# Maxima over pairs of PSUM banks in layer 0 of a two-layer cross-attention model, and a re-placed plan

## The chip, the core and the metric

One core of a Trainium2 chip runs the whole model. The metric is the device time of one launch in microseconds. TensorE (PE) multiplies, VectorE (DVE), ScalarE (ACT) and GpSimd (POOL) work on vectors, and SyncE's queue (SP) issues the transfers.

## The reference

`x` is 16 batches of 256 rows of 128; the context is 16 batches of 1601 rows. Two layers run one after the other, each with 16 heads of 8:

```python
x = x + self_attention(x)          # layer 0: causal; layer 1: given mask
x = x + cross_attention(x, ctx)    # 256 queries, 1601 keys; layer 1: given mask
x = x + mixture(x)                 # 8 experts, top 2, 128 -> 512 -> 128
# attention: softmax(q @ k.T / sqrt(8)) @ v, for each head
```

Layer 0 uses layer norms and exact GELU, layer 1 RMS norms, SiLU and one shared expert more.

## The kernel before

**What is computed where.** Every attention needs, for each query and head, the largest score, before the exponential. So the kernel computes the cross scores twice. First come the *maxima*: steps of kind MC, with queries in the 128 partitions. One matmul of 32 contraction rows gives the scores of one head, 128 queries and 512 keys: one full PSUM bank (`chunk_maxima`, L832). VectorE reduces that bank to one number per query (`vector_program`, L1075 in layer 0; in layer 1 a custom operation at L1081 adds the mask as well, followed by a read of its accumulator). The 1601 keys are three chunks of 512 and a tail of 68; a tail step holds both halves of the queries (L1077). A group of four heads has 2 x 3 x 4 = 24 full steps and 4 tails; four groups make a batch. NR (L1085) reduces the chunks to one maximum, NC (L908, L1068) turns it and puts it into a spare row of the query tensor, so that the second computation gives score minus maximum.

Second come the *scores*: a beat of four SC steps (four heads, keys in the partitions, L943, two matmuls each), which ScalarE exponentiates (L1232), and the sums WV (L961), 16 matmuls with the values. A group has 7 such beats, a batch 28.

**Row groups and waves.** The four heads of a group lie at partitions 0, 32, 64 and 96. Matmuls of different heads run side by side in TensorE, so a *wave* of several MC steps takes hardly longer than one. Heads come in the order 2, 3, 0, 1.

**Banks.** Seven PSUM banks, each a tensor of its own, are shared by everything; the eighth holds the sums. A step waits until the last reader of its bank is done (`wait_empty`).

**The plan.** Nothing is dynamic: before the program is emitted, `weave` lays out one order for all engines. A *round* t computes the scores of batch t and, beside them, as side work, the maxima, keys (KC, L990), values (VC, L996), projections (QP, L856) and self-attention (MS, SS) of batch t+1, the loads for t+2, and the experts (EF L1022, ES L1034) of batch t-1. Rounds 0 to 15 are layer 0's, 16 to 31 layer 1's. `WHEN` gives each kind of side work a begin and an end as fractions of `LENGTH`. At each step `weave` tries the head of every list on `Model`, a model of the engines' times, and takes the one with the least planned idle time plus `NEAR` times its place plus `HEAVY` times the backlog.

Maxima are no list of their own. Two places pull them: behind every beat of scores or self-attention, as many steps as the model finds free banks, at most `MOST` = 3, on condition that they are free within `SOON` (such steps are *led* and belong to that beat's wave); and, where `behind` says that the maxima lag the scores, one more beat of up to three after the scores' piece, whether the banks are free or not. `place` gives a step the bank that is free first. Every engine then runs its steps in that order; VectorE's ring of tiles is read in order of issue.

**The queue SP** issues the key moves KD (L1347, 12 transfers a group, 48 a batch), the experts' weights (L1359, two slots), contexts (L1325), masks (L1355), inputs (L1320) and stores (L1364), each after a wait for its buffer.

## Time and profile before

| | us |
|---|---|
| median of 3 runs | 4735.49 |
| lowest and highest | 4720.38, 4739.81 |
| profiled execution, span from first to last instruction | 4733.2 |
| TensorE, VectorE, ScalarE, GpSimd busy | 4551.8, 3608.6, 2701.6, 698.8 |
| mean granted clock of TensorE | 0.980 |

The time of the profiled execution as a launch is not given apart from its span, so what lies around the span is not known. In a group row, "busy" is the time in which at least one instruction of the group ran, "mean ns" the mean duration of one (overlapping ones count in full), and the last part tells how long the engine idled just before them and what ended it. In a timeline row, neighbouring instructions of one line are merged.

### The profile page before, as it was taken

The page shows a single profiled execution, that of the slowest core. Times are in us where ns is not written, and L with a number is a line of the kernel's source. Part 1 is how long each engine was busy: PE and PEld are TensorE (multiplying, and loading weights), DVE is VectorE, ACT ScalarE, POOL GpSimd, SP SyncE. Part 2 cuts the span into 40 slices and gives each one's busy share as a digit, 9 for nine tenths or more (in the row PEclk, how much of TensorE's full clock was granted, in tenths as well). Part 3 has the DMA queues.
Part 4 walks back from the last instruction along what each step waited for, and adds up shares of the span by engine and source line. Part 5 has one row for each costly group of instructions (what it writes and reads, how often), then busy time and mean ns, then how long its engine had stood idle before and what let it go on. Part 6 is the DMA issues. An engine that isn't in the chain of part 4 may idle for free.

```text
span 4733.2 us, 104936 instructions
## 1 busy us (share of the span) xinstructions
PE 4551.8 (96%) x40946; PEld 2800.6 (59%) x41312; DVE 3608.6 (76%) x9823; ACT 2701.6 (57%) x5505; POOL 698.8 (15%) x853
## 2 busy tenths in 40 slices
PE   6999999999999999999999999999999999999999
PEld 3566555666655566665565556655566555655566
DVE  6867777777777777777768887788877888788875
ACT  1666666667666666665565555555555555555554
POOL 2111211211121121111110111011110111101100
PEclk8999999999999999998999999999999999999999
DMA  2222222222222222223233323332233323333222
GB/s 68 39 60 57 44 55 56 63 67 56 60 46 53 55 65 67 53 58 80 55 97 81 83 61 87 96 86 68 66 99 82 86 61 83 103 81 80 62 70 74
DMA packets 168008, 327.22 MB, mean 69 GB/s; under 512 B 25656, under 2 KB 76624, under 8 KB 167520
## 3 DMA queue, kind: packets, MB, share of 16 engines
q1 hardware_dynamic: 167184, 320.48, 27.6%
q8 instruction: 333, 5.46, 0.5%
q14 instruction: 155, 1.27, 0.1%
q10 hardware_dynamic: 336, 0.01, 0.0%
HBM read 237.40 MB, written 4.19 MB: 51 GB/s over the span
## 4 chain that ended last, share of the span: by engine, by line
PE 79%; DVE 14%; ACT 3%; issue 2%; SPq 1%; DMA 0%; POOL 0%; DVEq 0%
PE sums L961 16%; PE b L1022 10%; PE b L1034 10%; PE b L832 9%; PE b L943 7%; PE b L933 7%; DVE chunk_max L1075 5%; PE b L856 4%; PE b L917 3%; DVE nm_s L1064 3%; DVE b L1081 3%; PE b L884 2%; PE b L996 2%; PE b L908 2%; ACT probs_c L1232 1%
## 5 line engine op out<-in xcount | busy, mean ns | idle before, releaser
L1232 ACT ACTIVATE probs_c<-b 128x512 f32<-128x512 f32 (+1 forms) x3584 | 1738.8, 571 | 1069.0 <-PE b L943 1061.2
L1081 DVE CUSTOM_DVE_ANT_0 b<-b,mcross_q 128x512 f32<-128x512 f32 (+1 forms) x2048 | 1121.8, 605 | 211.2 <-PE b L832 208.9
L1075 DVE TENSOR_REDUCE chunk_max<-b 128x1 f32<-128x512 f32 x1536 | 973.6, 683 | 144.3 <-PE b L832 139.3
L961 PE MATMUL sums<-probs_c,vc 128*32 128x256 f32 x13312 | 932.4, 395 | 0.6 <-ACT o_c L1236 0.3
L832 PE MATMUL b<-kc,qc 32*128 32x512 f32 (+1 forms) x4096 | 820.5, 412 | 18.2 <-DVE chunk_max L1075 7.1
L1034 PE MATMUL b<-w_back,hidden 128*128 128x128 f32 x4352 | 562.3, 280 | 14.7 <-DVE vc L1138 9.2
L832 PEld LDWEIGHTS b<-kc,qc 32*128 32x128 f32 x4096 | 425.3, 187 | 250.9 <-ACT probs_c L1232 94.4
L1034 PEld LDWEIGHTS b<-w_back,hidden 128*128 128x128 f32 x4352 | 526.4, 192 | 73.3 <-ACT probs_c L1232 24.4
L961 PEld LDWEIGHTS sums<-probs_c,vc 128*32 128x32 f32 x13312 | 348.0, 111 | 341.1 <-issue 168.0
L943 PE MATMUL b<-qc,kc 32*128 32x256 f32 (+1 forms) x6656 | 514.4, 336 | 16.7 <-DVE chunk_max L1077 2.2
L1022 PE MATMUL b<-xT_e,w_in 128*128 128x256 f32 x2176 | 527.9, 387 | 0.8 <-DVE chunk_max L1081 0.7
L1214 DVE SCALAR_TENSOR_TENSOR xe<-b,comb,xe 128x128 f32<-128x128 f32 x544 | 188.0, 349 | 405.3 <-PE b L1034 404.3
L943 PEld LDWEIGHTS b<-qc,kc 32*128 32x128 f32 (+1 forms) x6656 | 302.4, 182 | 300.2 <-issue 185.0
L1227 ACT ACTIVATE probs_s<-b 128x512 f32<-128x512 f32 x512 | 277.8, 594 | 308.1 <-PE b L895 305.7
L1022 PEld LDWEIGHTS b<-xT_e,w_in 128*128 128x128 f32 x2176 | 396.7, 191 | 88.1 <-ACT probs_c L1232 25.4
L933 PE MATMUL b<-mcross_k,ident_b 128*128 128x512 bf16 (+1 forms) x1569 | 403.1, 363 | 32.8 <-ACT probs_s L1227 11.1
L1064 DVE TENSOR_REDUCE nm_s<-b 128x2 f32<-128x512 f32 x512 | 328.5, 684 | 31.2 <-PE b L889 31.1
L1081 DVE DVE_READ_ACCUMULATOR2_ANT chunk_max<- 128x1 f32 x2048 | 290.7, 142 | 0.0
L933 PEld LDWEIGHTS b<-mcross_k,ident_b 128*128 128x128 bf16 (+1 forms) x1792 | 169.1, 99 | 201.5 <-DVE chunk_max L1081 37.9
L1207 DVE SCALAR_TENSOR_TENSOR hidden<-hidden,b 128x512 f32<-128x512 f32 x288 | 193.6, 686 | 101.4 <-ACT hidden L1255 101.4
L1307 POOL TENSOR_TENSOR rstd_s<-mean_var_s,halves 128x2 f32<-128x2 f32 x32 | 23.2, 724 | 1607.6 <-DVE mean_var_s L1122 1607.6
L1251 ACT ACTIVATE hidden<-b,b_hid 128x256 f32<-128x256 f32 x512 | 207.1, 474 | 88.5 <-PE b L1022 86.3
(159 smaller groups left out, 4498.6 us busy)
## 6 DMA issues: line engine op xcount, KB each, us to landing
w_in<-in_experts SPq DMA_DIRECT2D x272, 256.0 KB, 3.2
w_back<-in_experts SPq DMA_DIRECT2D x272, 256.0 KB, 3.3
kc<-k_hi SPq DMA_DIRECT2D x1024, 50.0 KB
ctxT<-in_ctxT SPq DMA_DIRECT2D x32, 800.5 KB, 6.2
kc<-k_lo SPq DMA_DIRECT2D x512, 50.0 KB
mask_words<-in_mcross SPq DMA_DIRECT2D x32, 800.5 KB
mask_words<-in_mcrossT SPq DMA_DIRECT2D x32, 768.0 KB
out_x<-xe SPq DMA_DIRECT2D x32, 128.0 KB, 1.9
```

Source lines behind the costliest of these rows:

```text
L832: last = pe.matmul(tile[:, n * y.kn:(n + 1) * y.kn], T["qc"][y.p][rows, y.g, qt * P:(qt + 1) * P], T["kc"][rows, y.g, y.k0:y.k0 + y.kn], s ...
L933: pe.matmul(tile_of(T, y)[0:y.kn, 0:n * S], T["ident_b"][0:y.kn, 0:y.kn], mask, start=True, stop=False)
L943: last = pe.matmul(tile_of(T, y)[0:y.kn, half * S:(half + 1) * S], T["kc"][rows, y.g, kt * P:kt * P + y.kn], T["qc"][y.p][rows, y.g, :], s ...
L961: last = pe.matmul(acc[HP * j:HP * j + HP, :], T["vc"][x.p][0:x.kn, v0:v0 + HP], probs_of(T, x)[0:x.kn, j, half:half + S], start=x.j == 0, ...
L1022: last = pe.matmul(tile[:, half * S:(half + 1) * S], T["w_in"][load.slot][:, f * P:(f + 1) * P], T["xT_e"][:], start=True, stop=True)
L1034: last = pe.matmul(tile[:, 0:D], hid[:, f, x.c * P:(x.c + 1) * P], T["w_back"][load.slot][:, f * D:(f + 1) * D], start=f == 0, stop=f == N ...
L1064: dve.tensor_reduce(maxima[:, x.j, :, MROW], tile.rearrange("p (q k) -> p q k", q=QT), AX, ALU.max, negate=True).then_inc(M["d_read"], 1)
L1075: done = dve.tensor_reduce(best[:, x.i:x.i + 1], tile, AX, ALU.max)
L1081: done = dve.tensor_tensor_reduce(part, part, mask, 1.0, -3e38, ALU.add, ALU.max, best[:, qt:qt + 1])
L1227: act.activation(T["probs_s"][:, x.j, :], tile, ACT.Exp, scale=SCALE).then_inc(M["a_read"], 1)
L1232: act.activation(probs_of(T, x)[0:x.kn, x.j, 0:n], tile[0:x.kn, 0:n], ACT.Exp, scale=SCALE).then_inc(M["a_read"], 1)
L1251: done = act.activation(T["hidden"][x.i % 2][:, f, :], tile[:, half * S:(half + 1) * S], ACT.Gelu, bias=T["b_hid"][:, x.i, f:f + 1])
```

## The change

In layer 0 an MC step covers two heads, 2 and 3 or 0 and 1, in two neighbouring banks: two matmuls of different row groups, and one reduction over both banks that writes two maxima; a tail step makes four matmuls and, still, two reductions. A group has 12 full steps and 2 tail steps for 24 and 4. All seven banks become one PSUM tensor, so that an instruction can address two of them. The planner counts tiles rather than steps: `MOST` becomes 4 tiles, for both layers; a led pair needs two free neighbours (`pairs_in`); `place` looks for two neighbouring banks; a pull made because nothing else can go on takes at most two tiles. Within a wave the matmuls go round by heads. Layer 1 keeps one bank a step (`TWO_BANKS` is false for it, and what is written for `WIDE` isn't reached). `LENGTH` of layer 1 goes from 145.8 to 130.4, `HEAVY` from 0.091 to 0.096, and the fractions of `WHEN` change in both layers; `SLACK` is 2 steps of 28 as before, now as a share.

```diff
+TWO_BANKS = (True, False)
...
-LENGTH = (140.4, 145.8)
+LENGTH = (140.4, 130.4)
...
     def place(self, x):
 
         taken = {n for y in x.beat[:x.beat.index(x)] for n in y.banks} if x.led else ()
-        return [min((n for n in range(BANKS) if n not in taken), key=lambda n: max(self.pe, self.banks[n]))]
+        width = tiles_of(x)
+        runs = [range(n, n + width) for n in range(BANKS - width + 1)]
+        return list(min((some for some in runs if not any(n in taken for n in some)),
+                        key=lambda some: max(self.pe, *(self.banks[n] for n in some))))
...
-NEAR, AHEAD, SOON, MOST, SLACK = 0.0436, 167.5, 0.32, 3, 2
-HEAVY, DRY = 0.091, 0
+NEAR, AHEAD, SOON, MOST, SLACK = 0.0436, 167.5, 0.32, 4, 0.07
+HEAVY, DRY = 0.096, 0.0000
...
-                more = plan.pull(model, pending, min(MOST, len(free)))
+                more = plan.pull(model, pending, min(MOST, len(free)), room=free)
...
+def maximum_us(x):
...
+    if TWO_BANKS[x.l]:
+        return 1.07 if x.c < CHUNKS else 0.45
+    return (0.6, 0.65)[x.l] if x.c < CHUNKS else 0.3
...
+def parts_of(x):
...
+    tails = x.c == CHUNKS
+    return [(x.j + n, qt, n * BANK + tails * qt * x.kn, x.k0, x.kn) for qt in (range(QT) if tails else [x.i])
+            for n in range(tiles_of(x))]
...
+                heads = (2, 0) if TWO_BANKS[l] else (2, 3, 0, 1)
...
-    def pull(self, model, pending, most, late=False):
-
-        out = []
-        while len(out) < most and self.groups:
+    def pull(self, model, pending, most, late=False, room=None):
+
+        out, taken = [], 0
+        while self.groups:
             x = self.groups[0][0]
+            taken += tiles_of(x)
+            if taken > most or taken > 2 and late:
+                break
             needs = [y for name, y in x.of.items() if name != "mask"]
+            if tiles_of(x) > 1 and room is not None and pairs_in(room) < len(out) + 1:
+                break
...
-WHEN = [{"experts": (0.207, 1.0), "keys": (0.177, 0.426), "values": (0.198, 0.975), "self": (0.08, 0.58), "load": (0.358, 1.0), "context": (0.95, 1.0)},
-        {"experts": (0.079, 1.0), "keys": (0.293, 0.368), "values": (0.119, 0.401), "self": (0.029, 0.629), "load": (0.5, 0.656), "context": (0.49, 0.668), "cross masks": (0.393, 0.779), "self masks": (0.786, 0.796)}]
+WHEN = [{"experts": (0.207, 1), "keys": (0.157, 0.426), "values": (0.313, 0.975), "self": (0.077, 0.577),
+         "load": (0.368, 0.988), "context": (0.929, 0.939)},
+        {"experts": (0.079, 1), "keys": (0.282, 0.368), "values": (0.119, 0.37), "self": (0.029, 0.584),
+         "load": (0.378, 0.623), "context": (0.469, 0.661), "cross masks": (0.333, 0.692),
+         "self masks": (0.772, 0.786)}]
...
+    turns = [(y, n) for n in range(len(parts_of(maxima[0]))) for y in maxima] if even else [
+        (y, n) for y in maxima for n in range(len(parts_of(y)))]
...
+            last = pe.matmul(T["psum"][:, first:first + kn], T["qc"][y.p][head_rows(j, HP), y.g, qt * P:(qt + 1) * P],
+                             T["kc"][head_rows(j, HP), y.g, k0:k0 + kn], start=True, stop=True)
...
+                heads = tiles_of(x)
+                two = T["psum"][:, first:first + heads * BANK].rearrange("p (j n) -> p j n", j=heads)
+                best = T["chunk_max"][:, x.g % 2, :, x.j:x.j + heads, x.c].rearrange("p q j -> p j q")
+                if tails:
+                    for j in range(heads):
+                        done = dve.tensor_reduce(best[:, j, :], two[:, j, 0:QT * TAIL].rearrange("p (q k) -> p q k", q=QT),
+                                                 AX, ALU.max)
+                else:
+                    done = dve.tensor_reduce(best[:, :, x.i], two, AX, ALU.max)
...
-        "banks": [psum(f"b{n}", [P, BANK]) for n in range(BANKS)],
+        "psum": psum("pool_of_banks", [P, BANKS * BANK]),
```

## Rows read from the trace of the kernel before

**Rows 1.** The page's head and its first part: busy time, share, instructions.

```profile
span 4733.2 us, 104936 instructions
...
PE 4551.8 (96%) x40946; PEld 2800.6 (59%) x41312; DVE 3608.6 (76%) x9823; ACT 2701.6 (57%) x5505; POOL 698.8 (15%) x853
```

**Rows 2.** Windows of 13 rounds of each layer: busy (count), PEclk, DMA share, GB/s.

```profile
349.00:2154.30 1805.30, 1744.35 (x15882) 1088.77 (x15947) 1325.74 (x2918) 1180.68 (x2394) 318.53 (x378) 0.97 0.25 57
2461.00:4426.90 1965.90, 1922.91 (x17404) 1170.82 (x17639) 1598.83 (x5048) 1013.22 (x2082) 245.27 (x313) 1.00 0.32 81
```

**Rows 3.** Windows of single rounds, two of layer 0 and the last.

```profile
630.20:766.80 136.60, 132.32 (x1225) 82.99 (x1230) 101.82 (x225) 90.78 (x185) 24.49 (x29) 0.99 0.26 58
905.00:1044.90 139.90, 135.49 (x1225) 84.11 (x1230) 102.11 (x225) 90.83 (x186) 24.48 (x29) 0.96 0.25 57
2154.30:2309.30 155.00, 147.58 (x1239) 91.73 (x1244) 109.63 (x276) 91.22 (x186) 26.18 (x34) 0.89 0.31 79
```

**Rows 4.** Windows around one dip of the clock.

```profile
919.00:922.40 3.40, 2.94 (x17) 1.64 (x13) 3.30 (x9) 0.13 (x1) 0.00 (x0) 1.00 0.00 0
...
925.90:929.20 3.30, 3.30 (x30) 2.36 (x32) 2.29 (x8) 1.41 (x3) 0.00 (x0) 0.51 0.00 0
```

**Rows 5.** The chain, 349 to 2154.3, by line.

```profile
by line: PE sums L961 17.1%; PE b L832 11.8%; PE b L1034 10.8%; PE b L1022 10.4%; DVE chunk_max L1075 9.6%; PE b L943 8.1%; PE b L856 4.3%; PE b L917 3.2%; DVE nm_s L1064 2.8%; PE b L884 2.0%; PE b L908 2.0%; PE b L996 1.9%; ACT probs_s L12
```

**Rows 6.** Groups by line and form, 349 to 2154.3: busy us, mean ns, idle before.

```profile
L1075 DVE TENSOR_REDUCE chunk_max<-b 128x1 f32<-128x512 f32 x1248 | 791.4, 683 | 110.1 <-PE b L832 105.5
...
L832 PE MATMUL b<-kc,qc 32*128 32x512 f32 x1249 | 323.2, 466 | 5.4 <-DVE chunk_max L1075 3.5
...
L1077 DVE TENSOR_REDUCE chunk_max<-b 128x2 f32<-128x136 f32 x208 | 52.9, 294 | 21.4 <-PE b L832 21.3
```

**Rows 7.** Waits of TensorE's loads, 349 to 2154.3: total us, times, longest.

```profile
PEld b L832 <- DVE chunk_max L1075: 47.5, 130, 0.5
...
PEld b L943 <- DVE chunk_max L1075: 16.3, 47, 0.4
PEld b L996 <- DVE chunk_max L1075: 14.8, 39, 0.4
```

**Rows 8.** VectorE's timeline from 1037 us: start, us, count.

```profile
1041.55 2.48 DVE L1075 TENSOR_REDUCE chunk_max<-b 128x1 f32<-128x512 f32 x4 [0.30 <-PE b L832]
...
1045.47 1.29 DVE L1075 TENSOR_REDUCE chunk_max<-b 128x1 f32<-128x512 f32 x2
```

**Rows 9.** TensorE's timeline in layer 1.

```profile
2900.29 0.39 PE L832 MATMUL b<-kc,qc 32*128 32x512 f32 x1
2900.61 1.07 PE L961 MATMUL sums<-probs_c,vc 128*32 128x256 f32 x16
2901.61 0.50 PE L832 MATMUL b<-kc,qc 32*128 32x512 f32 x4
2902.04 2.94 PE L1034 MATMUL b<-w_back,hidden 128*128 128x128 f32 x24
```

**Rows 10.** TensorE's timeline in layer 0.

```profile
968.12 0.72 PE L832 MATMUL b<-kc,qc 32*128 32x512 f32 x3
968.77 1.07 PE L961 MATMUL sums<-probs_c,vc 128*32 128x256 f32 x16
...
971.75 0.49 PE L832 MATMUL b<-kc,qc 32*128 32x512 f32 x1 [0.27 <-DVE chunk_max L1075]
```

**Rows 11.** The first and the last wave of those counted (690 with them).

```profile
349.45 0.63 PE L832 MATMUL b<-kc,qc 32*128 32x512 f32 x3
...
2152.45 0.50 PE L832 MATMUL b<-kc,qc 32*128 32x512 f32 x1
```

**Rows 12.** Waits of SP's queue, whole execution.

```profile
SPq L1359 <- PE b L1034: 491.5, 113, 10.5
...
SPq L1347 <- DVE chunk_max L1075: 341.7, 17, 25.4
```

**Rows 13.** DMA issues: size, median us to landing.

```profile
ctxT<-in_ctxT SPq DMA_DIRECT2D x32, 800.5 KB, 6.2
```

More of the change, by code:

```diff
@@ L59 @@
 TAIL = 68
+TWO_BANKS = (True, False)
+WIDE = 802
 CHUNKS = SK // BANK
@@ L210, in read @@
             idle = max(0, second - max(self.dve, made))
-            self.dve = max(self.dve, made, second) + (0.3 if kind == "MC" and x.c == CHUNKS else self.cost(DVE_US, x))
+            self.dve = max(self.dve, made, second) + (maximum_us(x) if kind == "MC" else self.cost(DVE_US, x))
             done = self.dve + PASS
@@ L253, in add @@
                 n = [y for y in x.beat if y.kind == "MC"].index(x)
-                self.pe = self.run(begin, WAVE if n % HG else 0.22 + (0.1 if first_wave else 0), 0.053)
+                wave = 0.34 if tiles_of(x) > 1 and x.l else 0.22
+                whole = HG // 2 if tiles_of(x) > 1 else HG
+                self.pe = self.run(begin, WAVE if n % whole else wave + (0.1 if first_wave else 0), 0.21 / whole)
             elif x.kind in ("SC", "MS", "SS"):
@@ L380, in __init__ @@
         self.at = {}
-        self.waiting, self.groups, self.follow, self.pulled = [], [], [], 0
+        self.waiting, self.groups, self.follow, self.pulled, self.share = [], [], [], 0, {}
         self.model = Model()
@@ L531, in pull @@
             out.append(self.groups[0].pop(0))
-            self.pulled += 1
+            self.pulled += self.share[id(out[-1])]
             if self.groups[0][0].kind == "NR":
@@ L537, in behind @@
     def behind(self, x):
-        steps = QT * HG * CHUNKS + HG
-        return self.pulled < steps * (self.batch * NG + x.g + 1 + (x.i + 1) / (KP - 1.5)) - SLACK
+        return self.pulled < self.batch * NG + x.g + 1 + (x.i + 1) / (KP - 1.5) - SLACK
     def scores(self, l, p, g, kp):
@@ L815, in tile_of @@
 def tile_of(T, x):
-    return T["banks"][x.banks[0]][:]
+    return T["banks"][x.banks[0]]
 def chunk_maxima(pe, T, M, x):
-    for y in x.beat:
-        if y.kind != "MC":
-            continue
-        if y is not x:
-            wait_empty(pe, M, y)
-        if "q" in y.of:
-            pe.wait_ge(M["q_made"], nth(y.of["q"]))
-            pe.wait_ge(M["kc_moved", y.g], 16 * MOVES * y.of["moved"].c)
-        tile, rows = tile_of(T, y), head_rows(y.j, HP)
-        for n, qt in enumerate([y.i] if y.c < CHUNKS else range(QT)):
-            last = pe.matmul(tile[:, n * y.kn:(n + 1) * y.kn], T["qc"][y.p][rows, y.g, qt * P:(qt + 1) * P],
-                             T["kc"][rows, y.g, y.k0:y.k0 + y.kn], start=True, stop=True)
-        last.then_inc(M["d_made"], 1)
+    maxima = [y for y in x.beat if y.kind == "MC"]
+    even = len({len(parts_of(y)) for y in maxima}) == 1
+    turns = [(y, n) for n in range(len(parts_of(maxima[0]))) for y in maxima] if even else [
+        (y, n) for y in maxima for n in range(len(parts_of(y)))]
+    if maxima:
+        for y, n in turns:
+            parts = parts_of(y)
+            if n == 0:
+                if y is not x:
+                    wait_empty(pe, M, y)
+                if "q" in y.of:
+                    pe.wait_ge(M["q_made"], nth(y.of["q"]))
+                    pe.wait_ge(M["kc_moved", y.g], 16 * MOVES * y.of["moved"].c)
+            j, qt, begin, k0, kn = parts[n]
+            first = y.banks[0] * BANK + begin
+            last = pe.matmul(T["psum"][:, first:first + kn], T["qc"][y.p][head_rows(j, HP), y.g, qt * P:(qt + 1) * P],
+                             T["kc"][head_rows(j, HP), y.g, k0:k0 + kn], start=True, stop=True)
+            if n == len(parts) - 1:
+                last.then_inc(M["d_made"], 1)
 def tensor_program(pe, T, M, order):
@@ L1071, in vector_program @@
                 dve.wait_ge(M["masks_made"], nth(x.of["mask"]))
-            some = [(x.i, tile)] if x.c < CHUNKS else [(qt, tile[:, qt * TAIL:(qt + 1) * TAIL]) for qt in range(QT)]
+            tails = x.c == CHUNKS and x.kn == TAIL
             best = T["chunk_max"][:, x.g % 2, :, x.j, x.c]
-            if x.l == 0 and x.c < CHUNKS:
-                done = dve.tensor_reduce(best[:, x.i:x.i + 1], tile, AX, ALU.max)
-            elif x.l == 0:
-                done = dve.tensor_reduce(best, tile[:, 0:QT * TAIL].rearrange("p (q k) -> p q k", q=QT), AX, ALU.max)
-            else:
-                for qt, part in some:
+            first = x.banks[0] * BANK
+            if x.l == 0:
+                heads = tiles_of(x)
[5 more added lines that the diff above has]
+                                                 AX, ALU.max)
+                else:
+                    done = dve.tensor_reduce(best[:, :, x.i], two, AX, ALU.max)
+            else:
+                for n, qt in enumerate(range(QT) if tails else [x.i]):
+                    part = T["psum"][:, first + n * x.kn:first + (n + 1) * x.kn]
                     mask = T["mcross_q"][x.p][:, qt, x.k0:x.k0 + x.kn]
@@ L1441, in program @@
         "pick": sb("pick", [P, QT, E0]), "comb": sb("comb", [P, QT, E0 + 1]), "combT": sb("combT", [E0, S]),
-        "banks": [psum(f"b{n}", [P, BANK]) for n in range(BANKS)],
+        "psum": psum("pool_of_banks", [P, BANKS * BANK]),
         "sums": psum("sums", [P, BANK]),
     }
+    T["banks"] = [T["psum"][:, n * BANK:(n + 1) * BANK] for n in range(BANKS)]
     for role in "se":
```

25 lines of the change are left out of this document (21 added, 4 removed).

## The prediction

> **What bounds the kernel now.** I read the page first, for the load of the engines: TensorE is busy 96% of 4733.2 us, VectorE 76% [rows 1]. A busy share doesn't say what TensorE's time consists of, so next I cut the execution into rounds (one batch's pass through one layer), using the fourth `o_c` copy of each batch as the mark. Thirteen steady rounds of layer 0 take 1805.3 us, 138.9 each, at a granted clock of 0.97; thirteen of layer 1 take 1965.9, 151.2 each, at 1.00 [rows 2]. So layer 0, where the new operation goes, is about 16 x 139 = 2222 us of the whole. Single rounds of layer 0 come in kinds: 136.6 us at clock 0.99, 139.9 at 0.96, and the round that prepares layer 1 takes 155.0 at 0.89 [rows 3]. Work and order are nearly the same in them, so some 3 us of a round hang on the clock. It falls in short stretches from 2.4 to 1.2 GHz: from 925.9 to 929.2 it is 0.51 of full speed, some us after a stretch in which TensorE had gaps (busy 2.94 of 3.40 us) [rows 4].
>
> Then I read who ends TensorE's time. In layer 0's chain the maxima's reduction L1075 holds 9.6%: 173 us of 13 rounds, 13.3 a round [rows 5]. It is busy 791.4 us there, 60.9 a round [rows 6], so about 22% of it lies on the path. TensorE's loads wait for it at many lines: 47.5 us in 130 waits before L832, 16.3 before the scores L943, 14.8 before L996 [rows 7]. Summed over those three, 6 us a round. TensorE is the bound, and it is held up by banks that VectorE hasn't freed; most of the rest is its own work.
>
> **The change, part by part.** A round of layer 0 has 96 full tiles (16 batches: 1536 reductions in all) and 16 tails.
>
> (a) *The reduction.* 96 reductions of 512 become 48 of 2 x 512; the 16 tail reductions stay (two operations a step). The trace has no read over two banks. In a run, single reductions follow each other every 0.60 us: four end in 2.48, two in 1.29 [rows 8]. The slope is (683 - 294) ns over (512 - 136) elements [rows 6], 1.035 ns each, so 512 more cost 530 ns: a pair costs 1.13 us in a run where two singles cost 1.20. VectorE gains 0.07 x 48 = 3.4 us a round. Bounds: crossing banks costs as much as starting anew or more (2 x 683 ns = 1.37 us, a loss of 8 us a round), or the whole fixed part of an instruction vanishes (294 - 136 x 1.035 = 153 ns, a gain of 7.3). I take 0.07, since the slope comes from the same operation on the same memory. With 22% on the path: **-0.75 us a round**.
>
> The rows show a fixed part for each instruction. The Trainium skill (Advanced Engine Details and Errata, TRN2 Errata) speaks of a bubble between instructions and says that one instruction may read several PSUM banks; VectorE: DVE Perf Modes, in its section on the errata, gives 120 cycles and one per element at 0.96 GHz for a read of PSUM, by which the pair saves 125 ns, 6.0 us a round for 3.4; on the path that would be another 9 us over 16 rounds. The trace's 683 ns stands beside that page's 658.
>
> (b) *Fewer waves.* Tiles of different row groups run side by side: a wave of four lasts 0.50 us and the next work begins 0.43 after its start, and the shortest step, with a wave of one, is 0.32 (2900.29 to 2900.61) [rows 9]; I take 0.33 for a wave. In the 13 rounds I counted 570 waves of full tiles (156 of one, 153 of two, 236 of three, 25 of four or five) and 120 of tails, the first at 349.45 and the last at 2152.45 [rows 11]; 324 follow scores, 129 follow self-attention's beats, 104 follow the sums L961. That is 44 + 9 = 53 waves a round. After the change a round has 56 steps of two tiles. Behind the 28 beats of scores, which hold four of seven banks, at most one pair fits, and only if two neighbours are free; before, 93 of those 324 waves found only one tile, so I give a pair to 60%: 17. Of the 10 self-attention beats I give 5 one. The other 34 steps go where the plan is behind, two pairs at a time: 17 waves. So 39 waves for 53: 14 x 0.33 = **-4.6 us a round**.
>
> (c) *Waits for banks.* Those two-pair waves need four of seven banks, each pair as neighbours, and they stand in TensorE's fixed order: behind one that waits are the next sums or experts, and behind those ScalarE's and VectorE's next tiles. There are 9 more such waves than the 8 now after L961. The nearest row is the wait of L832's load for a reduction, 47.5/130 = 0.37 us [rows 7]: **+3.3 us a round**. Bounds: 0, when the banks happen to be free, and a whole pair's 1.13 on each of the 17. Against that, the third tile of a wave often came late (968.12, a wave of three lasts 0.72 us against 0.50 for a wave of four [rows 9, 10]); such delay averages 0.20 us in the 129 three-tile waves behind scores, 2.0 us a round. A pair waits too, for its later bank, so I take half: **-1.0**.
>
> (d) *Layer 1* keeps its custom operation on one bank; only the limit of three tiles becomes four where the plan is behind. It has 143 waves behind L961 in 13 rounds, 11 a round; one more tile in each takes about 4 waves of three away: -1.3 us. The fourth bank must be waited for at one or two of the eleven (0.37 each): **-0.8 us a round**, with bounds -1.3 (no wait) and +2.8 (a wait at each, 4.1, less 1.3).
>
> (e) *Side work at other places.* Instruction counts stay: 4 key steps, 5 value steps, and masks and loads as before. The key move's 48 DMA issues a batch and the loads share SP's queue. SP waits long there already (L1347 for the maxima: 341.7 us in 17 waits; L1359 for the experts' matmuls: 491.5 in 113) [rows 12], and a DMA releases TensorE in none of the costly waits (the three of [rows 7] are VectorE's), so moved loads cost nothing while they stay a few us ahead. What queues behind a waiting load on SP is the next expert's weights, which have two slots. The context load of layer 0 moves to 0.929 but stays behind the last value step; it lands in 6.2 us [rows 13], and the next keys start at 0.157 of a round, 22 us later. Should that cover go, the price is up to those 6.2 us a round, behind KC and everything on TensorE. Layer 1's length 130.4 for 145.8 mainly scales all its places, and weighs planned idle time more against them. What these moves do to the waits and to the clock I can't read from rows: 0, with bounds from the two kinds of rounds: all at 136.7 us is -2.2 a round, all at 139.9 +1.0 [rows 3]; for layer 1 +-1.5 (1%, an estimate from the spread of layer-0 rounds, since its own are even).
>
> The sum: layer 0 -0.75 - 4.6 + 3.3 - 1.0 = -3.05 a round, x 16 = -49 us; layer 1 -0.8 x 16 = -13 us. The profiled execution has 4733.2 us of span, and what lies around it isn't shown; the median of the runs is 2.3 above it. 4733 - 62 + 2 = **4673 us**, 1.3% faster.
>
> **Rivals.** *Slower: the pairs starve the banks.* From seven single banks VectorE's work becomes three pairs and a leftover, and a pair comes free only when both halves are read. Scores take four singles, often one of each pair, and so leave no neighbours. For it: TensorE already waits 0.37 us a time for these readers, and the window at 971.75 shows a single tile after an idle 0.27 for L1075 [rows 10]. Against it: a pair in a run is freed no later than the second single was. It decides from a mean wait of w with 17w = 3.0 (the 8 waits now) + 4.6 + 1.0 + 0.75, w = 0.55 us. At 0.8 us layer 0 is +4.3 a round, +68 us; with layer 1 unhelped or delayed by up to 1.5 a round: 4800 to 4825. On top come clock losses: at 0.96 all over, +16. The skill's Perfetto Trace Analysis, Matmuls, asks that independent groups rotate through different banks so that evacuation overlaps; holding two at once goes against that; no row here shows a pair held, so it isn't decided.
>
> *No change:* pairs are pulled one at a time, so 53 waves stay about 50; (b) and (c) shrink to nothing, and what is left is 0.75 x 16 = 12 us and some of layer 1: 4715 to 4735. For it: TensorE is 96% busy and most of the waves cost it only a third of a us.
>
> *The change doesn't do what it says:* the read over two banks costs two reads, 1.20 to 1.37 us. Then VectorE works up to 8 us a round more, at 22% +1.8, and layer 0 gains about 1: 4715.
>
> *Better than forecast:* new places also remove the stretch after the router (from 968.77 to 971.75 TensorE has one set of sums and then waits for L1075 [rows 10]) and keep the clock up: another 2.2 x 16 = 35 us, and some of the 155.0 us round: 4620 to 4640.
>
> **How the numbers follow.** Forecast 0.46, better 0.10, no change 0.16, two reads 0.06, starved banks 0.22. About 0.5% (24 us) is what a measurement of this kernel can tell from no change. Most of the forecast and all of the better case lie beyond it: faster 0.55; the no-change and two-read cases and the rim of the forecast's: same 0.22; starved banks and a rest of unlucky places: slower 0.23. The range goes from the better case to the lower part of the starved one: 4615 to 4800. The likeliest case alone spans 4635 to 4710.
>
> **What would show it.** A pair near 1.2 us alone and 1.13 in a run; 768 of them; the share of L1075's successor in layer 0's chain below 9.6%; about 40 waves a round, many of four tiles; L832's busy time in 13 layer-0 rounds well below 323 us for full tiles; rounds near 136 us in layer 0 and 150 in layer 1. Wrong would be: waits before L832's successor above 0.55 us a time, more than 50 waves, rounds above 139, or a layer 1 that moves more than layer 0.

## The result and the profile after

The changed kernel takes 4958.27 us (median of 4; 4936.48 to 4988.18) against 4734.83: **slower by 4.8%**, ratio 1.0479, 95% interval 1.0433 to 1.0524. The profiled execution took 4988.18 us, its span is 4986.6. The page's head and busy row:

```profile
span 4986.6 us, 104446 instructions
...
PE 4665.8 (94%) x40938; PEld 2808.5 (56%) x41312; DVE 3562.2 (71%) x9055; ACT 2701.8 (54%) x5505; POOL 687.3 (14%) x853
```

VectorE works 46 us less than before, as meant; TensorE's share falls from 96% to 94%. Cut into the same rounds as [rows 2], with the fourth `o_c` copy as the mark:

```profile
378.00:2377.40 1999.40, 1850.64 (x15870) 1111.67 (x15939) 1288.61 (x2293) 1181.38 (x2393) 316.00 (x378) 0.91 0.23 52
2695.30:4677.80 1982.50, 1917.76 (x17404) 1159.38 (x17638) 1596.01 (x5046) 1011.54 (x2081) 236.19 (x314) 1.00 0.31 81
```

A layer-0 round takes 1999.4/13 = 153.8 us for 138.9, at a granted clock of 0.91 for 0.97; a layer-1 round 152.5 for 151.2. Of the 253 us between the two spans, the first 378 us (349 before) hold 29, these 13 rounds of layer 0 hold 194 and the 13 of layer 1 hold 17; the rest lies between and behind the windows. The chain of layer 0, against [rows 5]:

```profile
by line: PE sums L1023 14.4%; DVE chunk_max L1146 13.7%; PE pool_of_banks L893 9.6%; PE pool_of_banks L1084 9.3%; PE pool_of_banks L1096 9.3%; PE pool_of_banks L1005 8.3%; ACT probs_c L1303 4.9%; PE pool_of_banks L918 4.4%; DVE nm_s L1126 2
```

The reduction has grown from 9.6% of 1805 to 13.7% of 1999, from 13 to 21 us a round, though it is busy less. The groups, against [rows 6]:

```profile
L1146 DVE TENSOR_REDUCE chunk_max<-pool_of_banks 128x2 f32<-128x1024 f32 x623 | 742.8, 1222 | 255.5 <-PE pool_of_banks L893 254.2
...
L893 PE MATMUL pool_of_banks<-kc,qc 32*128 32x512 f32 x1246 | 263.0, 530 | 41.6 <-DVE chunk_max L1146 24.1 <-DVE k_lo L1203 5.7 <-ACT probs_c L1303 3.4
...
L1143 DVE TENSOR_REDUCE chunk_max<-pool_of_banks 128x2 f32<-128x136 f32 x208 | 51.3, 294 | 63.2 <-PE pool_of_banks L893 63.2
```

A pair takes 1222 ns, and TensorE's time in full maxima tiles fell from 323.2 to 263.0 us. I counted the waves as before: 488 for 690 in 13 rounds, 37.5 a round for 53, of which 195 have two tiles and 195 have four. The maxima got cheaper on TensorE, then, and the loss is where something else waits. The waits of layer 0 name it, against [rows 7]:

```profile
PEld pool_of_banks L1005 <- DVE chunk_max L1146: 72.5, 103, 1.6
...
PEld pool_of_banks L893 <- DVE chunk_max L1146: 63.1, 115, 1.0
...
PE pool_of_banks L1005 <- DVE chunk_max L1146: 42.1, 79, 1.2
```

Before, the loads of the scores (L943, now L1005) waited 16.3 us in 47 times for a reduction; now 72.5 in 103, and their matmuls 42.1 more. One such place, in TensorE's timeline and then in VectorE's:

```profile
1206.37 1.13 PE L893 MATMUL pool_of_banks<-kc,qc 32*128 32x512 f32 x4
1207.66 0.38 PE L946 MATMUL pool_of_banks<-causal_k,ident_b 128*128 128x512 bf16 x1 [0.16 <-ACT probs_c L1303]
...
1208.91 0.49 PE L893 MATMUL pool_of_banks<-kc,qc 32*128 32x512 f32 x2 [0.44 <-DVE chunk_max L1146]
...
1209.95 0.50 PE L893 MATMUL pool_of_banks<-kc,qc 32*128 32x512 f32 x2
...
1210.29 0.27 PE L1005 MATMUL pool_of_banks<-qc,kc 32*128 32x256 f32 x1
1211.08 0.50 PE L1005 MATMUL pool_of_banks<-qc,kc 32*128 32x256 f32 x7 [0.52 <-DVE chunk_max L1146]
```

```profile
1207.54 4.62 DVE L1146 TENSOR_REDUCE chunk_max<-pool_of_banks 128x2 f32<-128x1024 f32 x4 [1.74 <-PE pool_of_banks L893]
```

A wave of two pairs is done by 1207.5, and two more pairs follow at 1208.91 and 1209.95. VectorE reads the four pairs in 4.62 us, that is (4.62 - 1.22)/3 = 1.13 from start to start. The beat of scores issues its first matmul at 1210.29 and its second only at 1211.08, just after the third of these reads ends (1207.54 + 1.22 + 2 x 1.13 = 1211.02).

To compare kernels I use one sum, the *scores' time*: from each start of a scores matmul to TensorE's next start, per layer-0 round of the profiled execution. It is 15.6 us before and 25.0 after, +9.4, the largest single term of the 14.9 lost, but not the whole account. The maxima's time, the same sum for their matmuls, fell by 4.8 (25.6 to 20.8), so the rest of TensorE's work makes up the other 10.3. Of that, 3.6 are the sums, 27.9 to 31.5, which hardly ever wait and took longer, at the lower clock. Their rows, before and after:

```profile
L961 PE MATMUL sums<-probs_c,vc 128*32 128x256 f32 x4992 | 351.5, 401 | 0.0
```

```profile
L1023 PE MATMUL sums<-probs_c,vc 128*32 128x256 f32 x4992 | 378.7, 426 | 0.5
```

The windows tell it from the other side. TensorE idles (1805.3 - 1744.35)/13 = 4.7 us a round before and (1999.4 - 1850.64)/13 = 11.4 after. So 6.7 of the 14.9 us are idle time, of which 4.3 stand just before matmuls of the scores (0.7 to 5.0) and 2.7 just before those of the maxima (0.6 to 3.3); the other 8.2 are busy time that has become longer.

### The profile page after: what moved, and what is told of

It reads as the page before. It is cut to its first block, busy times and chain, and to the rows that moved or that the text cites. A ratio compares the mean times of both kernels' runs of the same rounds, so it can differ in the third digit from the quotient of the medians.

```text
span 4986.6 us, 104446 instructions
## 1 busy us (share of the span) xinstructions
PE 4665.8 (94%) x40938; PEld 2808.5 (56%) x41312; DVE 3562.2 (71%) x9055; ACT 2701.8 (54%) x5505; POOL 687.3 (14%) x853
## 3 DMA queue, kind: packets, MB, share of 16 engines
q14 instruction: 149, 1.22, 0.1%
## 4 chain that ended last, share of the span: by engine, by line
PE 68%; DVE 21%; ACT 4%; SPq 3%; issue 2%; DMA 2%; POOL 0%; DVEq 0%
PE sums L1023 14%; PE pool_of_banks L1084 9%; PE pool_of_banks L1096 9%; PE pool_of_banks L893 8%; DVE chunk_max L1146 7%; PE pool_of_banks L1005 7%; PE pool_of_banks L995 6%; DVE pool_of_banks L1151 5%; PE pool_of_banks L918 4%; DVE nm_s L1126 3%; ACT probs_c L1303 3%; SPq L1418 2%; PE pool_of_banks L979 2%; DMA mask_words<-in_mcrossT 2%; PE pool_of_banks L946 1%
## 5 line engine op out<-in xcount | busy, mean ns | idle before, releaser
L1303 ACT ACTIVATE probs_c<-pool_of_banks 128x512 f32<-128x512 f32 (+1 forms) x3584 | 1739.6, 572 | 1352.5 <-PE pool_of_banks L1005 1346.6
L1151 DVE CUSTOM_DVE_ANT_0 pool_of_banks<-pool_of_banks,mcross_q 128x512 f32<-128x512 f32 (+1 forms) x2048 | 1121.8, 605 | 265.0 <-PE pool_of_banks L893 262.8
L1146 DVE TENSOR_REDUCE chunk_max<-pool_of_banks 128x2 f32<-128x1024 f32 x768 | 914.5, 1221 | 327.6 <-PE pool_of_banks L893 325.9
L893 PE MATMUL pool_of_banks<-kc,qc 32*128 32x512 f32 (+1 forms) x4096 | 697.6, 435 | 57.8 <-DVE chunk_max L1146 32.8
L1005 PE MATMUL pool_of_banks<-qc,kc 32*128 32x256 f32 (+1 forms) x6656 | 576.4, 348 | 83.9 <-DVE chunk_max L1146 55.4
L1005 PEld LDWEIGHTS pool_of_banks<-qc,kc 32*128 32x128 f32 (+1 forms) x6656 | 335.2, 188 | 411.7 <-issue 196.9
L1096 PE MATMUL pool_of_banks<-w_back,hidden 128*128 128x128 f32 x4352 | 561.7, 280 | 3.4 <-DVE chunk_max L1151 1.8
L1096 PEld LDWEIGHTS pool_of_banks<-w_back,hidden 128*128 128x128 f32 x4352 | 530.7, 193 | 54.2 <-issue 21.4
L1084 PE MATMUL pool_of_banks<-xT_e,w_in 128*128 128x256 f32 x2176 | 539.1, 393 | 3.3 <-DMA w_in<-in_experts 2.6
L893 PEld LDWEIGHTS pool_of_banks<-kc,qc 32*128 32x128 f32 x4096 | 340.4, 194 | 311.1 <-ACT probs_c L1303 108.3
L1084 PEld LDWEIGHTS pool_of_banks<-xT_e,w_in 128*128 128x128 f32 x2176 | 401.4, 194 | 102.3 <-ACT probs_c L1303 34.1
L995 PE MATMUL pool_of_banks<-mcross_k,ident_b 128*128 128x512 bf16 (+1 forms) x1568 | 409.1, 364 | 47.9 <-DVE chunk_max L1151 17.5
L1378 POOL TENSOR_TENSOR rstd_s<-mean_var_s,halves 128x2 f32<-128x2 f32 x32 | 23.1, 722 | 1685.8 <-DVE mean_var_s L1193 1685.8
```

What stands on the lines that cost most here:

```text
L893: last = pe.matmul(T["psum"][:, first:first + kn], T["qc"][y.p][head_rows(j, HP), y.g, qt * P:(qt + 1) * P], T["kc"][head_rows(j, HP), y.g ...
L995: pe.matmul(tile_of(T, y)[0:y.kn, 0:n * S], T["ident_b"][0:y.kn, 0:y.kn], mask, start=True, stop=False)
L1005: last = pe.matmul(tile_of(T, y)[0:y.kn, half * S:(half + 1) * S], T["kc"][rows, y.g, kt * P:kt * P + y.kn], T["qc"][y.p][rows, y.g, :], s ...
L1084: last = pe.matmul(tile[:, half * S:(half + 1) * S], T["w_in"][load.slot][:, f * P:(f + 1) * P], T["xT_e"][:], start=True, stop=True)
L1096: last = pe.matmul(tile[:, 0:D], hid[:, f, x.c * P:(x.c + 1) * P], T["w_back"][load.slot][:, f * D:(f + 1) * D], start=f == 0, stop=f == N ...
L1146: done = dve.tensor_reduce(best[:, :, x.i], two, AX, ALU.max)
```

## The experiments

| run | ratio to before (95%) | layer 0: us a round, clock | scores' time | layer 1: us a round |
|---|---|---|---|---|
| before | 1 | 138.9, 0.97 | 15.6 | 151.2 |
| changed | 1.048 (1.043-1.052) | 153.8, 0.91 | 25.0 | 152.5 |
| e1 singles | 1.032 (1.029-1.036) | 147.2, 0.94 | 19.2 | 152.9 |
| e2 old places | 1.058 (1.056-1.061) | 154.1, 0.92 | 25.5 | 154.1 |
| e3 new places | 1.021 (1.019-1.024) | 142.1, 0.96 | 16.7 | 154.6 |
| e4 two reads | 1.056 (1.053-1.058) | 154.4, 0.92 | 25.7 | 152.9 |
| e5 four | 1.027 (1.025-1.030) | 142.9, 0.96 | 17.5 | 154.1 |
| e6b one pair behind | 1.151 (1.148-1.153) | 180.0, 0.84 | 25.8 | 156.5 |
| e7 half release | 1.043 (1.041-1.045) | 149.0, 0.95 | 24.1 | 152.5 |
| e8 price | 1.064 (1.061-1.066) | 153.6, 0.92 | 24.9 | 153.2 |
| e9 pairs where they fit | 1.003 (1.001-1.004) | 139.0, 0.98 | 15.9 | 151.3 |
| e10 filler | 1.053 (1.051-1.056) | 153.3, 0.93 | 27.1 | 152.5 |
| e11 two | 1.059 (1.057-1.061) | 151.0, 0.94 | 20.6 | 157.3 |
| e12 spread | 1.027 (1.025-1.029) | 146.2, 0.95 | 22.4 | 152.9 |
| e13 spread, half release | 1.031 (1.028-1.034) | 145.5, 0.96 | 22.1 | 152.5 |
| e14 four, led | 1.017 (1.014-1.020) | 143.7, 0.96 | 17.5 | 151.4 |
| e15 four, behind | 1.020 (1.017-1.024) | 142.9, 0.96 | 18.8 | 153.7 |
| e16 spread, old places | 1.053 (1.050-1.056) | 152.6, 0.89 | 23.1 | 154.5 |
| e17 masks late | 1.084 (1.082-1.087) | 151.6, 0.93 | 24.9 | 164.5 |
| e18 masks early | 1.002 (1.001-1.003) | 138.9, 0.97 | 15.6 | 152.1 |

The ratios come from all runs of a version, against the kernel before in the same session. The us a round, the clock and the scores' time come from one profiled execution each. That of the changed kernel was the longest of its four (span 4986.6, their mean 4958.7), so differences of one or two us a round between rows may be those of single executions.

### Taking the change apart: e1, e2, e3, e5

```diff
e1, in the changed kernel:
-TWO_BANKS = (True, False)
+TWO_BANKS = (False, False)
e2, in the changed kernel:
-LENGTH = (140.4, 130.4)
+LENGTH = (140.4, 145.8)
... and HEAVY and WHEN of before
e3, in the kernel before:
-LENGTH = (140.4, 145.8)
+LENGTH = (140.4, 130.4)
... and HEAVY and WHEN of the change
e5, in the kernel before:
-NEAR, AHEAD, SOON, MOST, SLACK = 0.0436, 167.5, 0.32, 3, 2
+NEAR, AHEAD, SOON, MOST, SLACK = 0.0436, 167.5, 0.32, 4, 2
```

> The changed kernel with one tile a step in layer 0 again (one reduction a bank); the new places, the limit of four tiles and the one PSUM tensor stay. Theory A (pairs starve the banks of the scores): layer-0 rounds fall from 153.8 back to 138 to 142 us, the clock there to 0.96 or more, total 4740 to 4800. Theory B (the new places do the harm): layer-0 rounds stay above 148 us, total above 4880.

> The changed kernel with the places, the layer length and the backlog weight of before; pairs and the limit of four stay. Theory A: layer-0 rounds stay at 150 us or more, total 4920 to 5000, layer 1 near 151 to 152 a round. Theory B: layer-0 rounds fall to 142 or less, total below 4820.

> The kernel before with nothing but the new places, length of layer 1 and backlog weight. Theory A: within 1% of before, 4700 to 4780. Theory B: most of the loss is here already, above 4860.

> The kernel before with a limit of four tiles for three, nothing else. Theory D (it is the number of banks that one wave takes from the scores, not the pair as such): layer-0 rounds 141 to 146 us, the scores' time a round above the 15.6 of before, layer 1 152.5 to 154.5, total 4810 to 4890. Rival (four tiles are harmless one bank at a time): 4710 to 4760.

Measured: e1 4889.67, e2 5011.55, e3 4832.21, e5 4854.28 us. Neither theory stands alone: each of e1, e2 and e3 misses part or all of both theories' ranges, while e5 lies within theory D's in every point. Along one path a layer-0 round goes 138.9, with new places 142.1 (e3), with the limit of four 147.2 (e1), with pairs 153.8 (changed). Along the other, with the limit of four 142.9 (e5), with pairs 154.1 (e2). So pairs cost 6.6 to 11.2 us a round, the limit of four 4.0 to 5.1, the places 3.2 with single tiles. What a part costs depends on the others: with pairs and the limit of four, layer 0 takes the same with the new places as with the old (153.8 and 154.1). The new places suit the pairs' plan: the total with pairs is 53 us better with them than without. e1's load waits for a reduction before the scores lie between both kernels:

```profile
PEld pool_of_banks L1005 <- DVE chunk_max L1146: 45.8, 101, 0.8
```

e3 in the two windows of 13 rounds shows how much a mere re-placing costs in both layers:

```profile
347.20:2193.90 1846.70, 1775.16 (x15939) 1089.72 (x15939) 1323.69 (x2918) 1181.17 (x2393) 318.29 (x378) 0.96 0.24 56
2502.90:4512.60 2009.70, 1950.58 (x17638) 1160.80 (x17642) 1600.68 (x5047) 1012.63 (x2081) 236.82 (x314) 0.99 0.30 80
```

### What a pair does: e4, e7, e9

```diff
e4, in the changed kernel:
-                    done = dve.tensor_reduce(best[:, :, x.i], two, AX, ALU.max)
+                    for j in range(heads):
+                        done = dve.tensor_reduce(best[:, j:j + 1, x.i], two[:, j, :], AX, ALU.max)
e7, on top of e4 (for tails too); wait_empty waits for the count of the bank's own read:
+                        if j:
+                            done.then_inc(M["d_read"], 1)
e9, in the kernel before; banks are one tensor:
+            if x.joined:
+                continue
+            if x.mate:
+                two = T["psum"][:, first:first + 2 * BANK].rearrange("p (j n) -> p j n", j=2)
+                done = dve.tensor_reduce(T["chunk_max"][:, x.g % 2, x.i, x.mate.j:x.j + 1, x.c], two, AX, ALU.max)
```

> The changed kernel, the same order and the same pairs, but each pair read by two reductions of one bank each, the count of reads raised by the second alone. If the read over two banks is slow in itself (theory C): faster than the changed kernel by over 0.5%. Theory A: VectorE pays 0.06 us more a pair, 48 pairs a round, and so up to 1 us a round: total 0 to 20 us above the changed kernel's 4958.

> As the run with two reads for a pair (5000.6 us), the same order, but each of the two reads frees its bank at once. Theory E (a pair's first bank is held for the second's read, and that is what TensorE waits for): 40 us or more off 5000.6, to 4960 or less. Rival (TensorE waits for the last tile of a wave anyway): 4985 to 5010.

> The kernel before with its order of instructions on TensorE unchanged; the seven banks are one PSUM tensor, and where two heads' tiles of one wave can lie in neighbouring banks (177 times) one reduction reads both and frees both. The read itself is then priced without a new plan: VectorE gains 177 x 0.06 = 11 us, of which a fifth may show. All theories that blame the plan or the number of banks: 4715 to 4745, no change. If one tensor or the read over two banks were harmful in itself: above 4755.

Measured: e4 5000.58 us, e7 4934.31, e9 4750.93. The one read beats two by 42 us, twice the expected bound, so theory C falls. (In the table the two differ by only 0.6 us a layer-0 round, since the changed kernel's profiled execution is its longest.) With TensorE's order unchanged, freeing each bank at its own read takes 66 us off e4, 5.4 a layer-0 round, as theory E says. The scores' waits for reductions, e4 first, then e7:

```profile
PEld pool_of_banks L1005 <- DVE chunk_max L1147: 88.8, 124, 1.7
...
PE pool_of_banks L1005 <- DVE chunk_max L1147: 49.1, 82, 1.3
```

```profile
PEld pool_of_banks L1013 <- DVE chunk_max L1159: 56.4, 132, 1.0
...
PE pool_of_banks L1013 <- DVE chunk_max L1159: 19.0, 62, 0.7
```

88.8 + 49.1 becomes 56.4 + 19.0 (the rows of loads and matmuls overlap, so it is their fall that counts). This is the joint release, shown against two reads. The 5.4 us are not all in the scores' time, which fell by 1.6 (25.7 to 24.1); the sums fell by 1.8, and the windows, e4 first, give 12.3 and 9.4 us a round of idle TensorE at clocks of 0.92 and 0.95:

```profile
385.80:2393.50 2007.70, 1847.74 (x15938) 1106.69 (x15937) 1326.27 (x2917) 1183.31 (x2393) 317.40 (x378) 0.92 0.23 52
```

```profile
386.20:2323.20 1937.00, 1814.39 (x15940) 1101.10 (x15939) 1325.81 (x2916) 1182.97 (x2393) 316.76 (x378) 0.95 0.24 53
```

Against the changed kernel, with its one read, e7 gains 24 us, with intervals that overlap. e9 has TensorE's order of before, with the banks of the maxima chosen anew, and 177 pairs in all:

```profile
L1112 DVE TENSOR_REDUCE chunk_max<-pool_of_banks 128x1 f32<-128x512 f32 x984 | 632.8, 683 | 90.0 <-PE pool_of_banks L863 85.1
...
L1110 DVE TENSOR_REDUCE chunk_max<-pool_of_banks 128x2 f32<-128x1024 f32 x132 | 160.8, 1218 | 26.0 <-PE pool_of_banks L863 24.6 <-PE pool_of_banks L939 1.4
```

1218 ns a pair, VectorE busy a little less, and no gain: 15 us slower, 0.13 to 0.43%, just above the range expected. The read is not the harm (e4 says the same for the changed kernel's order), but neither is its saving worth anything here; what costs the 15 us, the read or the other choice of banks, isn't known.

### Smaller waves, and pairs at other places: e6b, e8, e11, e12, e13, e16

```diff
e6b, in the changed kernel, where the plan is behind:
-            steps = plan.pull(model, pending, MOST)
+            steps = plan.pull(model, pending, 3)
e8, in the changed kernel, the planner's price:
-        return 1.07 if x.c < CHUNKS else 0.45
+        return 1.15 if x.c < CHUNKS else 0.52
e11, in the kernel before:
-NEAR, AHEAD, SOON, MOST, SLACK = 0.0436, 167.5, 0.32, 3, 2
+NEAR, AHEAD, SOON, MOST, SLACK = 0.0436, 167.5, 0.32, 2, 2
e12, in the changed kernel:
-        if scores and plan.behind(scores[-1]):
+        plan.latest = scores[-1] if scores else plan.latest
+        pairs = plan.groups and tiles_of(plan.groups[0][0]) > 1
+        if (scores or pairs and plan.latest) and plan.behind(plan.latest):
             follow()
-            steps = plan.pull(model, pending, MOST)
+            steps = plan.pull(model, pending, 3 if pairs else MOST)
e13: e12 on top of e7. e16: e12 with the places, length and HEAVY of before.
```

> The changed kernel, but where the plan is behind it pulls at most three tiles, so one pair in layer 0 instead of two. Theory D: the scores wait less (25.0 us a round falls below 20), layer-0 rounds at most 148, total below 4890. Rival (any pair starves the banks, by its two neighbours): layer-0 rounds stay above 151, total 4930 or more.

> The changed kernel with the planner's price of a pair raised from 1.07 to 1.15 us and of a tail pair from 0.45 to 0.52, near what the trace shows (1.14 from start to start, 0.51). Theory F (the plan is bad because it takes a pair for cheaper than it is): 50 us or more below 4958. Theory D: the price hardly matters, 4920 to 4990.

> The kernel before with a limit of two tiles for three. If only the banks taken from the scores count (theory D alone), layer 0 gets faster: below 138.9 us a round. If there is an optimum, because smaller waves are more waves and the maxima fall behind, rounds go to 141 us or more and the total above 4790. I expect the second.

> The changed kernel, but where layer 0's maxima are behind the plan pulls one pair after every piece of work, scores or not, instead of two pairs after the scores alone. So no wave that isn't led takes four banks, and the slots suffice. Theory D: the scores' time falls from 25.0 to below 20 us a round, layer-0 rounds to 148 or less, total below 4900. Rival (a pair anywhere delays what comes next): total 4930 or more.

> The spread pairs of the run before (4868 us, 146.2 us a layer-0 round), and each pair read by two reductions that free their banks one by one. In the changed kernel's order that was worth 5.4 us a round against two reads with a joint release. Theory E: it is worth 2 to 5 here too, total 4800 to 4845. Rival (with no wave of four tiles, nobody waits for a pair's first half): 4860 to 4890.

> The run with spread pairs (4868 us) with the places, length and weight of before. With two-pair waves the old places cost 53 us against the new, nearly all in layer 1; one tile at a time they save 97. If the new places suit pairs: 4900 to 4950. If they only suit waves of four: below 4850.

Measured: e6b 5435.98 us, e8 5024.71, e11 5018.92, e12 4868.07, e13 4875.43, e16 4982.99. e6b missed on both theories. With one pair behind each beat there are too few places for 56 steps: 26 waves of its 13 rounds hold 8 or 10 full tiles, where the steps left over come one after another, and the maxima themselves become the wait:

```profile
PEld pool_of_banks L893 <- DVE chunk_max L1146: 214.9, 333, 2.1
...
PE pool_of_banks L893 <- DVE chunk_max L1146: 94.9, 143, 2.0
```

310 us in 13 rounds for L893 (loads and matmuls, partly the same time); in the changed kernel the loads waited 63.1. It tells nothing of starved scores, only that pairs need slots. e12 gives the slots with few waves of four: among waves of full tiles alone 51 in 13 rounds for 195, and 8 larger ones. It gets 90 us back, 7.6 a round. The total is as theory D says; the scores' time, 22.4, fell less than the 20 it asked for, as waits moved to the maxima:

```profile
PEld pool_of_banks L895 <- DVE chunk_max L1148: 94.5, 173, 1.5
...
PEld pool_of_banks L1007 <- DVE chunk_max L1148: 41.0, 60, 1.7
...
PE pool_of_banks L895 <- DVE chunk_max L1148: 27.0, 57, 1.3
...
PE pool_of_banks L1007 <- DVE chunk_max L1148: 24.2, 40, 1.4
```

e13 differs from e12 by the half release and by two reads for one, so it stands against e12 as e7 stands against the changed kernel: e7 is 24 us faster, e13 7 us slower (by the ratios 0.5% and 0.3%, both at the rim of the noise). That speaks for a joint release that hurts where four banks are queued for VectorE at once and not among single pairs. It isn't shown: the saving of the one read, 42 us among waves of two pairs, is in both comparisons, and single pairs with two reads and a joint release were not run. e11 shows the other side of the optimum, as expected: with two tiles 65 waves a round and 151.0 us. e8 (a true price made the plan worse by 66 us) rejects theory F, but lies above theory D's 4990 as well: the price mattered, and why isn't known. e16 says that the new places suit pairs, one or two at a time: without them 115 us more, above both ranges.

### Where the fourth tile does its harm: e14, e15

```diff
e14, in the kernel before:
-                more = plan.pull(model, pending, min(MOST, len(free)))
+                more = plan.pull(model, pending, min(4, len(free)))
e15, in the kernel before:
-            steps = plan.pull(model, pending, MOST)
+            steps = plan.pull(model, pending, 4)
```

> The kernel before, with four tiles allowed in the waves that ride on a beat of scores or self-attention, three elsewhere. Three banks at most are free behind a beat of four, so the limit of four rarely bites: 4725 to 4770.

> The kernel before, with four tiles allowed only in the waves of their own that are pulled when the maxima are behind. Theory D puts the 126 us of the limit of four here: 4810 to 4880. Rival (the loss is that of any other order, wherever the fourth tile goes): this and its sister lose about alike.

Measured: 4807.86 and 4826.19 us. I expected next to nothing of e14, and it lost 81 us with waves of almost the same sizes as before:

```profile
356.10:2224.50 1868.40, 1765.95 (x15871) 1089.10 (x15934) 1327.57 (x2919) 1179.70 (x2393) 317.63 (x378) 0.96 0.24 56
```

143.7 us a round in layer 0, layer 1 unhurt. e15 lost 100 us, within both theories' ranges, and 81 + 100 is more than the 126 of e5, so the two places don't add up. Theory D explains at most part of the limit's cost; a slightly other order of layer 0 costs 3 to 5 us a round by itself (e3, e5, e14, e15), at a clock of 0.96 for 0.97. What in those orders does it I haven't found.

### The clock: e10

```diff
in the changed kernel, scores of layer 0:
+                        if not x.last and y in scores[2:]:
+                            pe.matmul(tile_of(T, x)[0:x.kn, 0:S], T["kc"][head_rows(x.j, HP), x.g, kt * P:kt * P + x.kn],
+                                      T["qc"][x.p][head_rows(x.j, HP), x.g, :], start=True, stop=True)
                         wait_empty(pe, M, y)
```

> The changed kernel; in layer 0 TensorE repeats the first matmul of a beat of scores before it waits for the third and the fourth bank (54 repeats of 0.11 us a round, 6 us where nothing hides them). Theory G (TensorE's gaps bring the clock down, and the clock brings 0.6 us per us lost): the clock in layer 0 rises from 0.91 to 0.93 or more, and the total is at most 4975. Rival (the clock doesn't follow such gaps): clock within 0.01 of 0.91, total 4990 to 5050.

Measured: 4989.12 us.

```profile
386.60:2379.20 1992.60, 1857.54 (x16575) 1145.09 (x16574) 1287.12 (x2294) 1181.71 (x2392) 315.16 (x376) 0.93 0.23 52
```

The profiled clock in layer 0 is 0.93, as theory G says, but the total isn't, and it lies 1 us below the rival's range. Over all runs the granted clock of the whole kernel is 0.958 against 0.956, and the time is 31 us longer. So filling these waits in this way doesn't bring the clock back; the rise in layer 0 compares two single executions, of which the changed kernel's has the lowest clock of four. What the clock costs can be read without it, from executions of one kernel that differ in nothing else. The changed kernel's four spans are 4986.6, 4951.0, 4962.3 and 4934.9 us at clocks of 0.947, 0.957, 0.957 and 0.963. Call (1 - clock) x span the lost clock time: a fit within each kernel and session, over all kernels' executions up to e16 (114), gives 0.63 us of span per us lost. The changed kernel loses 218 us on average, the one before 94: 124 x 0.63 = 78 of the 223 us go with the clock, and some 145 would be there at an equal clock. This is an estimate. It carries what goes together within one kernel over to the difference between two, and takes the clock for the cause. In the profiled execution, at 0.947, the same rule gives 107 of its 253 us. What lowers the clock isn't shown by a run of its own; in the table it is mostly lower where rounds are longer.

### Layer 1: e17, e18

The chain of one layer-1 round of the changed kernel passes through the queue SP and a transfer:

```profile
3088.46 1.16 SPq L1418
3089.61 0.04 issue
3089.66 5.14 DMA mask_words<-in_mcrossT
3094.82 0.32 DVE mcross_k L1219
```

In this round the mask's load is issued only once the key moves (L1418) ahead of it in the queue are out. VectorE, which takes its work in order, waits for it, and TensorE's scores behind VectorE:

```profile
3094.82 0.96 DVE L1219 TENSOR_SCALAR mcross_k<-mask_words 128x1536 bf16<-128x1536 int32 x1 [1.22 <-DMA mask_words<-in_mcrossT]
...
3097.34 0.81 PE L995 MATMUL pool_of_banks<-mcross_k,ident_b 128*128 128x512 bf16 x3 [1.12 <-DVE xe L1285]
```

```profile
DVE mcross_k L1219 <- DMA mask_words<-in_mcrossT: 11.3, 13, 2.1
```

```diff
e17, in the changed kernel:            e18, in the kernel before:
-"cross masks": (0.333, 0.692)          -"cross masks": (0.393, 0.779)
+"cross masks": (0.439, 0.871)          +"cross masks": (0.298, 0.619)
```

> The changed kernel with layer 1's cross masks put back to the time of before (0.439 to 0.871 of 130.4 is 0.393 to 0.779 of 145.8). In the changed kernel VectorE waits 0.87 us a layer-1 round for a mask's load, and TensorE's scores wait behind it (9.8 us in 12 of 13 rounds). Theory M (the moved masks make layer 1's 1.3 us): no wait for that load, layer-1 rounds 151.2 to 151.9 instead of 152.5, total 10 to 25 us lower. Rival (the order as a whole): layer-1 rounds 152.3 or more.

> The kernel before with only the cross masks moved ahead to the time of the changed kernel. Theory M: the wait for the mask's load appears, 0.8 to 1.3 us a round, layer-1 rounds 152.0 to 152.8, layer 0 untouched at 138.9, total 4745 to 4765. Rival (any change of the order costs what the others cost): layer-1 rounds above 153.5.

Measured: e18 4743.8 us, 0.06 to 0.28% above before and 1 us below theory M's range, with layer 0 at 138.9 and layer 1 at 152.1, as theory M says. A wait for a mask's load is there, though for another mask than in the changed kernel. Before and in e18:

```profile
DVE mself_q L1148 <- DMA mask_words<-in_mself: 5.1, 10, 0.9
```

```profile
DVE mself_q L1148 <- DMA mask_words<-in_mself: 22.0, 12, 2.1
```

That is 1.3 us a round more on VectorE, for 0.9 in the round. e17, 5139.45 us, is no longer the same computation, its output is off by 3.6%. I take it that the late masks fall into the time in which layer 1 still uses others; that isn't shown. Its order of layer 1 is another too (164.5 us a round). It tells nothing of theory M, whose proof in the changed kernel stays open.

## Why the prediction was wrong

**Right.** (a) The pair's price: 1.13 us from start to start, and 1222 ns alone. (b) The waves: 37.5 a round for a forecast of 39. TensorE's time from a maxima matmul to its next start went from 25.6 to 20.8 us a round, -4.8, even at a lower clock. (d)'s count held too: layer 1 has 45 waves a round for 49. The rival "the pairs starve the banks" is part of what happened; it had a chance of 0.22 and stopped at 4825. It isn't all: with single tiles (e1) the new plan is still 3.2% slower.

**The step that failed is (c), waits for banks.** It charged +3.3 us a round before the two-pair waves, at 0.37 each, and nothing at the beat of scores that comes after them, though the text had named that beat as the taker of four of seven banks. There the runs show +9.4 us (25.0 for 15.6), of which 4.3 are TensorE's idle time before the scores' matmuls and part of the rest is the lower clock. The wait before a wave was near right (2.7 us more idle time before the maxima's matmuls, for 3.3); the wait behind it was left out. The price I used, of a wait for one bank's reader, was the wrong row for a beat that needs four banks while up to four are queued for VectorE: its longest single wait is 1.6 us in the waits of the loads. e7 shows what the joint release does: with two reads a pair it costs 5.4 us a round, 1.6 of them in the scores' time. I had dismissed it with "a pair in a run is freed no later than the second single was": true of the second bank, not of the first.

**The clock** was a term of the bounds only, +16 us at 0.96. It fell to 0.91 in layer 0, and some 78 us of the whole go with it by the fit above; for the profiled execution the same rule gives 6 to 7 us a layer-0 round. I took the clock of the rounds of before as its range, and the changed kernel left that range.

**(e), the moved work at nothing, failed as well.** With nothing else changed it costs 97 us (e3), 3.2 a round in layer 0 and 3.4 in layer 1. "Moved loads cost nothing while they stay a few us ahead" fell in layer 1: a load moved ahead in the plan was issued behind twelve-fold key moves in SP's queue, and TensorE waited for it across VectorE. VectorE's wait is 0.9 us a round; that it makes the 1.3 us of layer 1 isn't shown. For layer 0 the source of the 3 to 5 us that each other order costs is open. (d) forecast -0.8 from the limit of four in layer 1, and its sign depends on the places: with the old ones the limit costs 2.9 a round (e5), with the new ones, which the changed kernel has, it takes 1.7 off (154.6 in e3, 152.9 in e1).

The likely size of each part in layer 0 along the path by e3 and e1: places 3.2, limit of four 5.1, pairs 6.6, sum 14.9 us a round. By e5 and e2 the same 14.9 are limit 4.0, pairs 11.2, places -0.3. So the sizes hold only in their order; that pairs are the largest part holds in both. None of the versions beats the kernel before; the best of those with pairs in layer 0's plan is e12, 132 us above it.

## What to carry to other kernels

When an instruction claims several buffers at once, price the next taker of those buffers, and not only the instruction's own wait; ask how many of them are free when a beat that needs four comes. One read for two banks saves a twentieth of two reads and holds the first bank for the time of the second, and where four banks queued for the reader that ate up the saving: two reads that free their banks one by one were 66 us faster than two with a joint release, and no slower than the one read. In a plan written out by hand, count a re-placing as a change with a price of its own, and follow each moved load through the queue that issues it.

## What was not expected of the hardware

The granted clock differs between executions of one and the same kernel (0.947 to 0.963 for the changed one), and 0.63 us of span go with each us of lost clock time, by the fit over 114 executions. Repeating matmuls of 32 rows in the waits left the kernel's clock where it was (0.956 and 0.958).
